# Weight loads of a fused attention and feed-forward kernel queued ahead of the row loads at seven stage ends, and three gates at the phase change renamed

## The reference, cut to what matters

```python
def attn(x, Wqkv, bqkv, Wproj, bproj, gamma):          # x: (16, 2048, 1024) float32
    q, k, v = split(x @ Wqkv + bqkv)
    a = softmax((q @ k.T / sqrt(1024)) * mask)         # mask: gamma**(i-j) in 128-blocks on the diagonal, 1 elsewhere
    return (a @ v) @ Wproj + bproj
def ffn(x, w_gate, w_up, w_down):                      # int weights, scale 1/127, hidden 3072
    return (silu(x @ w_gate.T / 127) * (x @ w_up.T / 127)) @ w_down.T / 127
x = x + attn(layernorm(x), ...)
y = x + ffn(layernorm(x), ...)
```

## Time and profile before

| what | us |
|---|---|
| median of the timed runs | 6316.56 |
| the two timed runs | 6217.22 and 6415.91 |
| the profiled execution, its own time | 5445.35 |
| span of the slowest core (core 1) in it | 5443.8 |
| shortest span of the eight cores | 5431.9 |
| TensorE busy in the span | 4935.1 (91%) |

### The profile page before, as it was taken

How to read it: one execution, slowest core, us unless ns; L and a number is a source line. 1 busy time by engine, 2 the same in 40 slices (tenths; PEclk the granted TensorE clock), 3 DMA queues, 4 the chain that set the end, 5 groups by cost and what they waited for, 6 DMA issues and landing times.

```text
span 5443.8 us, 54549 instructions; the slowest of 8 cores (5431.9 to 5443.8 us)
## 1 busy us (share of the span) xinstructions
PE 4935.1 (91%) x22794; PEld 2299.0 (42%) x22794; DVE 1023.3 (19%) x1281; ACT 698.1 (13%) x1056; POOL 83.5 (2%) x123
## 2 busy tenths in 40 slices
PE   2899999987999989999899985999999999999999
PEld 1344444443444444444444442444444444444444
DVE  3222222211111121111111111111111111111111
ACT  2111111110001110001110011111111111111010
POOL 0110000000000000000000000000000000000000
PEclk9999999998999999999999997999999999999999
DMA  4562111125000010400010105121212121212121
GB/s 151 100 104 71 66 62 62 51 74 181 24 24 24 24 35 24 147 24 24 24 35 24 24 20 124 59 70 55 74 52 77 55 72 52 74 51 78 51 70 35
DMA packets 264248, 332.81 MB, mean 61 GB/s; under 512 B 129348, under 2 KB 170308, under 8 KB 262982
## 3 DMA queue, kind: packets, MB, share of 16 engines
q1 hardware_dynamic: 153126, 203.48, 13.0%
q0 software_dynamic: 63776, 58.73, 5.3%
q10 hardware_dynamic: 47104, 67.12, 3.4%
HBM read 260.06 MB, written 100.66 MB: 66 GB/s over the span
## 4 chain that ended last, share of the span: by engine, by line
PE 86%; DMA 7%; DVE 3%; issue 2%; ACT 1%; SPq 0%; DVEq 0%; ACTq 0%; POOLq 0%
PE ps L218 40%; PE ps L743 12%; PE ps L1024 12%; PE ps L643 12%; PE ps L801 6%; PE ps L703 1%; DMA x1A<-x_scr 1%; DVE x1t L808 1%; DVE x1t L812 1%; PE ps L353 1%; DMA wtmp<-wqkv 1%; DMA wubuf<-wu_scr 1%; DMA v_lo<-v_scr 1%; DMA q_scr<-qf_hi 1%; DMA k_hi<-k_scr 1%
## 5 line engine op out<-in xcount | busy, mean ns | idle before, releaser
L643 PE MATMUL ps<-k_hi,qt_hl 128*128 128x512 bf16 x2048 | 476.7, 384 | 30.8 <-DMA k_hi<-k_scr 26.9
L218 PE MATMUL ps<-xn2f_hi,wgbuf 128*128 128x512 bf16 x1536 | 374.5, 388 | 72.0 <-DMA wubuf<-wu_scr 72.0
L1024 PE MATMUL ps<-wd_sb,hf_hi 128*128 128x512 bf16 x1536 | 350.1, 390 | 20.8 <-DVE hf_lo L988 20.8
L218 PE MATMUL ps<-xn2f_lo,wgbuf 128*128 128x512 bf16 x1536 | 363.9, 380 | 0.0
L218 PE MATMUL ps<-xn2f_hi,wubuf 128*128 128x512 bf16 x1536 | 362.8, 379 | 0.0
L218 PE MATMUL ps<-xn2f_lo,wubuf 128*128 128x512 bf16 x1536 | 362.8, 379 | 0.0
L1024 PE MATMUL ps<-wd_sb,hf_lo 128*128 128x512 bf16 x1536 | 336.7, 379 | 0.0
L743 PE MATMUL ps<-v_hi,at_hi 128*128 128x512 bf16 x1024 | 324.5, 400 | 1.6 <-DMA v_lo<-v_scr 1.6
L743 PE MATMUL ps<-v_lo,at_hi 128*128 128x512 bf16 x1024 | 319.7, 395 | 0.0
L643 PEld LDWEIGHTS ps<-k_hi,qt_hl 128*128 128x128 bf16 x2048 | 201.7, 99 | 278.2 <-issue 41.5
L981 DVE SCALAR_TENSOR_TENSOR h<-ps,sgb 128x512 f32<-128x512 f32 x192 | 132.7, 691 | 960.3 <-PE ps L218 960.3
(11 more groups left out here) (113 smaller groups left out, 3857.5 us busy)
## 6 DMA issues: line engine op xcount, KB each, us to landing
wgbuf<-wg_scr SPq DMA_DIRECT2D x192, 256.0 KB, 2.7
wubuf<-wu_scr SPq DMA_DIRECT2D x192, 256.0 KB, 3.1
xsA<-x SPq DMA_DIRECT2D x32, 512.0 KB, 4.1
qt_hl<-q_scr SPq DMA_DIRECT2D x32, 512.0 KB, 8.0
xres<-x SPq DMA_DIRECT2D x32, 512.0 KB, 5.2
x_scr<-x1t POOLq DMA_DIRECT2D x32, 512.0 KB, 7.4
x1A<-x_scr SPq DMA_DIRECT2D x32, 512.0 KB, 4.8
y<-outA ACTq DMA_DIRECT2D x32, 512.0 KB, 5.0
```

The lines of the kernel that those rows point to most:

```text
L218: e.matmul(psum_ap, l, r, start=st, stop=sp),
L643: kb=kb, st=first, sp=last: e.matmul(ps0[:, kb * 512:kb * 512 + KW], lhs, kx[:, dc * S + kb * KW: dc * S + (kb + 1) * KW], start=st, stop=sp),
L1024: e.matmul(psd[:, half * 512:(half + 1) * 512], lhs, wd_sb[:, hc * D + half * 512: hc * D + (half + 1) * 512], start=st, stop=sp),
```

## The change

Four edits are made.

1. The load of `w_down` waits for `t_scmm_last`, the last score matmul of phase B, instead of for `endB`.
2. The four row loads of stage 0 wait for `t_p1tok[31]`, the first VectorE step of the last group's output, and load `j` for the store of its own row block, instead of all for all 32 stores.
3. The first weight loads of stage 0 also wait for the last attention-times-v matmul.
4. After the down half of each stage but the last, the loads of chunks 0 and 1 of the next stage are emitted, and so stand in SP's list ahead of the next `emit_x1_loads`. The old place finds them already in `t_wld` and skips them.

```diff
+            x1st[g] = t_st
...
+        t_scmm_last = t_scmm[NG - 1]
+        t_avmm_last = t_avmm[NG - 1]
...
         t_wd = P("gpsimd", lambda e: e.dma_start(out=wd_out, in_=wd_in),
-                 waits=endB, inc="g_cv", dma=True)
+                 waits=[t_scmm_last], inc="g_cv", dma=True)
...
-            g0 = [("s_sx1", plan.cnt["s_sx1"])] if u == 0 else []
...
-                waits=g0 + [t_xn2.get((u - 2, j)), t_oev.get((u - 2, j))],
+                waits=([t_p1tok[NG - 1], x1st[j]] if u == 0 else
+                       [t_xn2.get((u - 2, j)), t_oev.get((u - 2, j))]),
...
-                            gw = [("g_cv", n_cv)]
+                            gw = [("g_cv", n_cv), t_avmm_last]
...
+            for hh in ((0, 1) if u + 1 < NST else ()):
+                if hh >= HC or (u + 1, hh) in t_wld:
+                    continue
+                pw = hh % 2
+                gw = [t_wmm.get((u, HC - 2 + hh))]
+                tg = P("sync", lambda e, hh=hh, pw=pw: e.dma_start(
+                    out=wgbuf[:, pw * D:(pw + 1) * D].rearrange(
+                        "p (c h) -> p c h", c=DC),
+                    in_=wg_scr[hh]),
+                    waits=gw, inc="s_lwg", dma=True)
+                tu = P("sync", lambda e, hh=hh, pw=pw: e.dma_start(
+                    out=wubuf[:, pw * D:(pw + 1) * D].rearrange(
+                        "p (c h) -> p c h", c=DC),
+                    in_=wu_scr[hh]),
+                    waits=gw, inc="s_lwu", dma=True)
+                t_wld[(u + 1, hh)] = [tg, tu]
```

More of the change, by code:

```diff
@@ L677, in build_program @@
         t_s2done = [None]
+        x1st = {}
         prefetch_q(0)
```

## The result

The ratio of the changed kernel to the kernel before is 0.9881, with a 95% interval of 0.9864 to 0.9897: 1.2% less time, within the 2% that was set as the bound for "the same". The profiled execution took 5384.45 us against 5445.35 us before, 60.9 us less; the forecast made against it was 5382.8 us.

What follows compares the result with a forecast made beforehand. The prediction took the kernel as bound by TensorE, busy 4935.1 of 5443.8 us. Terms 48.4 + 10.2 + 4.0 = 62.6 us, subtracted from the 6316.56 us median, gave 6254.0 us, range 6129 to 6379 us; profiled, 5382.8 us.

Steps and rivals of the forecast that it cites:

- The stage ends: Phase C: moving weight loads ahead of row loads removes six TensorE pauses of 8.07 us each, 48.4 us.
- The slow matmuls: First matmuls after each of six stage-end pauses: full clock instead of half saves 1.70 us each, 10.2 us.
- The phase change: Start of phase C: row loads and the w_down load start earlier, 4.0 us gained, bounds -0.2 and 4.8.
- Chunk 2's room: Next stage's start: chunk 2's load has 6.9 us, needs 5.56 us at most, so costs nothing.
- The median: Timed runs of the whole kernel: 6316.56 us less the same 62.6 us gives 6254.0 us, 1.0% less.
- Rival E: Whole kernel: timed runs fall elsewhere, a median can lie 130 us off; low side 6190 us or less, chance 0.17.
- A: Stage ends keep a wait because another condition ends the pause; 17 us lost, 6271 us, chance 0.07.
- C: Without stage-end pauses, stages are stretched by 16% throughout, up to 248 us lost; 6502 us, chance 0.04.
- D: Phase change: the large load begun earlier delays the rows, -0.2 us instead of 4.0; 6258 us, no separate chance.
- B: Stage-end pauses paid for themselves in timed runs through faster matmuls; 19 us given up, 6273 us, chance 0.10.

Runs made afterwards that it cites:

- edit 4 alone: Kernel before with only the next stage's chunk 0 and 1 weight loads moved ahead of the row loads; ratio 0.988, profiled 5384.53 us.
- the filled pause: Kernel before with 36 unread matmuls added in each of six stage-end pauses; ratio 0.9972, profiled 5430.66 us.
- the gates alone: Kernel before with edits 1 to 3 only, without the moved weight loads; ratio 0.9992, profiled 5442.17 us.
- the second run of the changed kernel: Changed kernel with all four edits, run again beside the kernel before; seven runs between 5399.32 and 6147.81 us, no ratio.
- the kernel with half of the move: Kernel before with only chunk 0's pair of weight loads moved ahead of the row loads; ratio 0.9897, profiled 5395.18 us.
- the first experiments: Early follow-up runs, not listed one by one, with the kernel before timed beside them: median 5451.87 us over 19 runs.
- the kernel with all three further edits: Changed kernel plus early w_down load, first weights ahead of row loads, statistics chain freed of the last store; fastest execution 5350.67 us, no ratio.
- the kernel with the row loads' gate alone: Kernel before with edits 2 and 3 only, w_down load still waiting for endB; timed runs 5674.94 to 6358.68 us, no ratio.

## Why the prediction was right or wrong, point by point

**The stage ends, 48.4 us: right.** The pause of 8.1 us is gone at all six, the seventh stage end is unchanged, and edit 4 alone gives the ratio of the whole change. Reading the one stage end that already lacked the row loads was enough to price the others, and the stage periods are 254.9 to 256.6 us, where 256.5 us was forecast.

**The slow matmuls, 10.2 us: right.** The six starts run at full clock now, and the filled pause shows that this term exists without the other. On top came 3.4 us that was not forecast: two down halves lost their slow start. The sum for phase C was 58.6 us; 62.0 us were measured on the slowest cores and 61.4 us in the mean of the eight. One sentence of the prediction was too narrow: that such a change can only win time in which TensorE isn't busy. Its busy time fell too, from 4935.1 to 4916.9 us, as slow matmuls count as busy.

**The phase change, 4.0 us: about right in size.** The profile of the slowest cores gives 3.8 us; the means over eight cores give 2.1 us for the changed kernel, 3.0 us with the gates alone and 4.5 us in the second run of the changed kernel. That the large load would start only some 3 us earlier because of its place on the GpSimd queue was right. That the row loads would keep part of their earlier start, and lose part to the large load beside them, was right too (4.9 us won, 1.5 us lost). Whether the start of the large load has a part in it isn't decided: with and without edit 1 the phase change takes 60.3 us, in one execution each. What the prediction did not look for is how much room the term had: 28 us, behind the one queue entry that it named.

**Chunk 2's room: right.** Nothing waits there, and in the kernel with half of the move a load beside the same transfers needed at most 4.9 us.

**The median: wrong, and this is the step that failed.** The prediction says: "What stretches them is in no row. The removed pauses are DMA and queue time, so I subtract the same 62.6 us: 6254.0 us". The 62.6 us hold where both kernels run at the level of the profile (60.9 us between the two profiled executions); the number that they were taken from, 6316.56 us, was not the level of the kernel. It was a median of two runs, both 14% or more above the profiled execution. The runs since show both kernels between 5382 or 5444 us and over 6300 us: beside the first experiments the kernel before has a median of 5451.87 us over 19 runs. Rival E allowed for a shift of 130 us from the spread of the two runs; the shift was 868 us. The 871 us between profile and median were written down and should have been in the width of the range, from 5383 us at the low end. The relative change of the profiled time was forecast at 1.15% less, and the ratio measured is 1.2% less.

What stretches an execution is in rows of later traces: the granted clock. In the second run of the kernel with all three further edits, stretches of core 0 and then of core 3, another core of the same die:

```profile
2800.00:3000.00 200.00, 180.51 (x834) 86.93 (x848) 34.90 (x42) 19.27 (x30) 1.60 (x3) 0.97 0.09 24
3400.00:3600.00 200.00, 195.83 (x740) 82.65 (x754) 25.56 (x33) 17.02 (x27) 0.00 (x0) 0.81 0.16 50
```

```profile
800.00:1000.00 200.00, 197.55 (x773) 84.89 (x772) 39.58 (x57) 30.02 (x46) 0.00 (x0) 0.81 0.13 43
2000.00:2200.00 200.00, 187.02 (x713) 81.04 (x712) 28.75 (x35) 16.18 (x24) 1.06 (x2) 0.78 0.06 16
2800.00:3000.00 200.00, 182.69 (x850) 86.84 (x849) 34.90 (x42) 19.28 (x30) 1.60 (x3) 0.97 0.09 24
```

On core 0 the clock falls as phase C begins, from its usual 0.97 in phase B. On core 3 it is low in phase A already and rises again in the middle of phase B.

Phase C takes 2479.8 us on core 0 and 2051.9 us on core 4, whose clock is 0.98 to 1.00 there. The other two cores of that die go with these, core 1 with core 0 and core 2 with core 3. What sets off such a stretch, and how often it comes, stays open. Nothing here shows that the change has a part in it, and the experiment meant to test it gave no ratio.

**The rivals.** A (a wait remains) and C (slower) did not happen. Of D, the row loads beside the large load are slower, but by 1.5 us and not by 5. B (the pauses pay for themselves in the stretched executions) finds nothing in the one trace that has such pauses at the lowered clock. It is the kernel with the row loads' gate alone, core 2, at the end of stage 5. The granted clock is 0.81 before the pause, and behind it:

```profile
5051.32 3.57 PE L218 MATMUL ps<-xn2f_hi,wgbuf 128*128 128x512 bf16 x8 [7.95 <-DMA wubuf<-wu_scr]
5054.69 2.40 PE L218 MATMUL ps<-xn2f_lo,wgbuf 128*128 128x512 bf16 x8
5056.91 2.27 PE L218 MATMUL ps<-xn2f_hi,wubuf 128*128 128x512 bf16 x8
```

Eight matmuls take 1.89 us at a clock of 1.00. Here they take 3.57, 2.40 and then 2.27 us, and the granted clock of 5055 to 5100 is 0.81 again. Core 3 shows the same. The pause gives no stretch of faster matmuls back; whether the change saves the same 61 us in such executions was not measured.

The page of the Trainium skill, TensorE: Matmul & The Clock Gate, in its part on the clock gate, says that a die is held to 13/16 of the clock, 0.81, once three of its cores run dense matmuls, and for as long as the load lasts. The value agrees with the stretches above. The rest does not: with all eight cores at work the profiled executions near 5350 to 5450 us have a granted clock of 0.956 to 0.973 over the span, and the cores of one die have their stretches of 0.81 at different times, one of which ends in the middle of phase B.

## What to carry to other kernels

In a queue that is played strictly in order, look at what stands ahead of a load that comes late, not at the load's own conditions: its buffer was free for more than 80 us here, and moving it ahead of four row loads was all of the gain that the timed runs show. The same holds the other way: loosening a wait brings no more than the instructions ahead in the queue allow. Counted from the start of L808 or its like, the change issued the large load 3.1 us earlier; with its place in the list changed it was issued another 44 us earlier, and 28 us were won. And where a profile and the timed runs lie far apart, forecast the ratio and keep the range of the absolute time as wide as that gap.

## What the runs showed of the hardware that was not expected

- Filling six pauses of 8 us with matmuls that nobody needs makes the kernel faster by 0.28% (0.15 to 0.41%). The matmuls behind them take 1.89 us for eight and not 3.57 us, at the upper clock of 2.4 GHz, and most down halves lose their slow start as well.
- The same pause of at most 2.7 us before a down half drops the granted clock in most stages (0.52 to 0.64 over the next 3.5 us) and not in others (1.00), worth 1.7 us each time. On the slowest cores none of the eight is spared before, and two after; with the filler five to seven are, on six of the cores.
- One large casting load on the GpSimd queue slowed loads from SP's queue by a factor of 2 to 3: 512 KB from 3.2 us to 8 to 10 us, and 256 KB from 3.1 us to as much as 10.7 us. The load itself took 51.0 us beside them and 42.7 us before them.
- Within one execution the granted clock of some cores of a die is 0.81 for hundreds of microseconds and 0.97 to 1.00 before or after, under the same work. An 8 us pause did not end such a stretch on the two cores that show one. It makes phase C 2479.8 us long and not 2051.9 us.
